# A selective-scan layer with a quantized feed-forward on one core: one order per chunk of a sequence, and bulk transfers issued behind the first chunk's C rows

## The chip, the cores and the metric

The kernel runs on 1 core of one Trainium2 chip. The metric is device time in microseconds (us), as the median of several executions. Four engines compute: TensorE (PE, with its weight loads shown apart as PEld), VectorE (DVE), ScalarE (ACT) and GpSimd (POOL). SyncE (SP) issues most of the DMAs. Each engine works through its own instruction list strictly in order; they meet only at semaphores.

## The reference, cut to what matters

The input x is 8 sequences of 2048 rows of 512 numbers.

```python
x = x + s6(layernorm(x))          # state space layer, 16 states per channel
#   xp = h @ x_proj_w.T           -> d_rank (64), B (16), C (16) for each row
#   delta = softplus(d_rank @ dt_proj_w.T + dt_proj_b)
#   for each state n:  s = exp(delta*A[n]) * s + delta*B[n]*h    (serial along the rows)
#   y = sum_n s_n * C[n]  + h * D
x = x + ffn(layernorm(x))         # int8 quantized matmul
#   x_scale = max|h| / 127 ; q = round(h / x_scale) ; out = (q @ weight_q.T) * x_scale * weight_scale + bias
```

## The kernel before

The 16384 rows are cut into 32 chunks of 512 rows, four to a sequence. A chunk's second step is 16 units, one for each state n; chunk p has units 16p to 16p+15. A unit goes through the engines like this:

- ACT (`decay`, L611) writes exp(delta*A[n]) into one of seven buffers A0 to A6, four pieces of 128x512. Unit s uses buffer A(s mod 7), which names the unit in the rows below.
- The term delta*B[n]*h is made with channels on partitions in one of three PSUM banks PB. For 10.5 of the 16 states ACT scales rows into DB (`act_b`, L632) and PE transposes them (`tb`, L777). For states 2, 5, 8, 11, 14 and half of 15, PE multiplies with a diagonal matrix DG (`tb`, L774), which is read back from a scratch tensor b_diag in device memory: SP writes B into its diagonals (`store_g`, L410) and loads them (`load_g`, L418). Off the diagonals b_diag is zero, written once at the start (L445).
- DVE (`scan`, L932) runs the recurrence over A in four pieces. In chunks 1 to 3 of a sequence it starts from CAR, the last column of the chunk before, which ACT copies (`carry`, L618); in chunk 0 it starts from zero, and after chunk 3 there is no copy.
- POOL (`times_c`, L546) multiplies the unit by C[n], broadcast to all partitions in CB. CB is loaded by SP for four states at once (`load_c`, L397) from c_rows, where `store_c` (L390) has put the chunk's C.
- PE (`th`, L799) transposes the unit back and adds it into Y.

Around these run the first layernorm and projections of the next chunk (`stats0`, `aggr0`, `log0`, `shift0`, `xn`, `x_t`, `xt_out`, `x_p`, `xp_out`, `b_c`, `bc_out`, `d_t`, `delta`, `dl_t`, `du`), and the second layernorm, quantization and matmul of the chunk before (`gather`, `square`, `var1`, `amax`, `root`, `inv`, `ascale`, `scales`, `step`, `centre`, `turn`, `qt_out`, `q_mm`, `scale_a`, `scale_p`, `add_c`). `add_b` and `add_c` are DMAs of POOL that add into the output.

The order on every engine is a table of numbers. `place` gives each task of chunk p the number 1000p plus its entry in PLACES; FIRST replaces the first entries for chunk 0, LAST those of chunk 31; `run` sorts. So all chunks but the first and last share one order, whatever their place in the sequence.

Before `run`, SP issues the loads of the first rows and weights, X1, two zero fills of b_diag (L445, 1.5 MB each), the quantized weights in two halves into C and DB2 (L449), ws, bias, its copy and X2. DVE's `weights` (L913) waits for all four of s_w2 and casts both halves.

Of the kernel before, what the change touches and what calls it, by code (L numbers as in the profile page):

```python
# [5 lines left out]
PERIOD = 1000  # L6
PLACES = {
        "act_b": (-188, -188, -123, -123, -121, -31, -25, -25, -10, 30, 38, 52, 143, 163, 166, 167, 167, 213,
        213, 235, 235, 235, 244, 244, 268, 308, 344, 344, 344, 441, 474, 531, 563, 588, 588, 595, 598, 625,
        626, 626, 714, 793),  # L10
        "add_b": (1370,),
        "add_c": (2141,),
        "aggr0": (-1339,),
        "amax": (1290,),
        "ascale": (1401,),
        "b_c": (-481,),
        "bc_out": (-526,),
        "bias_p": (20000, 20001, 20002, 20003),
        "carry": (60, 183, 215, 237, 251, 287, 314, 355, 468, 582, 651, 651, 693, 730, 916, 1005),
        "centre": (1446, 1465, 1481, 1481),  # L20
        "d_t": (-440, -423, -404, -391),
        "decay": (-248, -248, -229, -229, -45, 3, 10, 10, 92, 117, 136, 136, 136, 138, 151, 189, 192, 192,
        200, 200, 200, 200, 200, 200, 200, 200, 200, 241, 247, 247, 247, 265, 323, 323, 331, 331, 331, 331,
        369, 394, 439, 439, 439, 439, 549, 549, 549, 567, 641, 641, 654, 654, 658, 658, 658, 665, 665, 665,
        671, 671, 682, 684, 684, 727),
        "delta": (-428, -410, -395, -374),
        "dl_t": (-317, -149, -133, -122),
        "du": (-35, -33, -32, -30),
        "gather": (1172, 1172, 1173, 1173),
        "idle": (2244, 2663, 2696, 3192),  # L30
        "inv": (1291,),
        "last_p": (25000, 25001),
        "last_q": (885, 1247, 1323, 1493),
        "last_v": (30000, 30001),
        "load": (-2254,),
        "load_c": (91, 545, 545, 706),
        "load_g": (-320, -16, -2, 187, 679, 680),
        "log0": (-1232,),
        "put_last": (30000, 30001, 30002, 30003),
        "put_x": (1260,),  # L40
        "q_mm": (1883, 1894, 1928, 1946),
        "q_t": (201, 1218, 1342, 1469),
        "qt_out": (1825, 1825, 1937, 1937),
        "root": (1336,),
        "rstd0": (-1188,),
        "scale_a": (1948, 1973, 1982, 2042),
        "scale_out": (20000, 20001, 20002, 20003),
        "scale_p": (2083,),
        "scales": (1293,),
        "scan": (-9, -9, -9, 171, 171, 171, 171, 171, 171, 171, 171, 171, 172, 186, 212, 212, 212, 215, 215,  # L50
        215, 215, 215, 215, 215, 215, 215, 273, 281, 286, 289, 290, 292, 292, 292, 376, 376, 532, 532, 540,
        555, 592, 617, 617, 660, 660, 660, 661, 661, 668, 668, 866, 921, 921, 922, 922, 922, 962, 965, 967,
        969, 972, 972, 972, 984),
        "shift0": (-999,),
        "square": (1298, 1298, 1298, 1305),
        "stats0": (-2032, -2028, -2022, -1604),
        "step": (1442,),
        "store_c": (-276,),
        "store_g": (-322,),
# [8 lines left out]
        "times_c": (-187, 121, 353, 361, 361, 375, 404, 432, 442, 630, 763, 763, 763, 804, 808, 808),  # L68
        "turn": (1884,),
        "var1": (1317,),  # L70
        "weights": (-475,),
        "x_p": (-506, -503, -503, -487),
        "x_t": (-567, -557, -540, -531),
        "xn": (-783, -777, -767),
        "xn_p": (-641,),
        "xp_out": (-632,),
        "xt_d": (-1484, -1483),
        "xt_out": (-746, -725, -697, -692),
# [3 lines left out]
        "act_b": (-16343, -15473, -15469, -15107, -13275, -13273, -13174, -8291, -7133, -6341, -4257, -2015),  # L82
        "aggr0": (-3608,),
        "b_c": (-14522,),
        "bc_out": (-19425,),
        "carry": (-9543, -214),
        "d_t": (-14199, -14195, -13844, -13844),
        "decay": (-16453, -15024, -14020, -13332, -13332, -13332, -10585, -8244, -8243, -6057, -4718, -3029),
        "delta": (-19425, -18068, -18034, -18034),
        "dl_t": (-13844, -13844, -13844, -13844),  # L90
        "du": (-987, -941, -941, -665),
        "load": (16363,),
        "load_c": (-13005, -6878, -2125, -1821),
# [65 lines left out]
def build(nc, cs, dg, b4, x, a_log, d_skip, wxp, wdt, dt_b, wq, ws, bias, out):  # L159
# [36 lines left out]
    with ctx:  # L196
# [844 lines left out]
```

## Time and profile before

| | us |
|---|---|
| median of 3 runs (2790.3 to 2793.21) | 2790.7 |
| the profiled execution | 2791.34 |
| its span, first to last instruction | 2789.6 |
| busy in the span: PE / DVE / ACT / POOL | 2746.0 / 2711.7 / 2694.8 / 2689.7 |
| PE weight loads busy | 2516.2 |
| instructions PE / DVE / ACT / POOL | 22516 / 2801 / 4927 / 980 |
| mean granted TensorE clock | 0.996 of full speed |
| moved by DMA | 344.33 MB, mean 123 GB/s |

In the 40 slices of the span all four engines stand at nine tenths or more from the second slice to the last but one. A row of waits names the engine that waited and its line, then what released it, with the total, the count and the longest. In a timeline row the bracket is the idle time ahead of the group and its releaser. PE's busy time has modelled ends, so a PE that is always busy need not be at its full pace.

### The profile page before, as it was taken

To read this page: it belongs to the slowest core of one execution; us is meant where nothing else is said; L and a number is where in the kernel's file an instruction comes from. 1 tells how busy PE (TensorE), PEld (TensorE's weight loads), DVE (VectorE), ACT (ScalarE), POOL (GpSimd) and SP (SyncE) were. 2 spreads that over 40 slices of the span, in tenths; PEclk is the share of its full clock that TensorE was granted. 3 is DMA by queue.
4 is the path that set the end of the run, shared out by engine and by line. 5 is a ranking of instruction groups with operands and counts; after the bars stand their busy time and mean duration, and the time that the engine had idled before them with its cause. 6 is when DMAs were issued, how large, how long until landed. Compare 5 with 4: busy or idle time off the path is not lost.

```text
span 2789.6 us, 59136 instructions
## 1 busy us (share of the span) xinstructions
PE 2746.0 (98%) x22516; PEld 2516.2 (90%) x22516; DVE 2711.7 (97%) x2801; ACT 2694.8 (97%) x4927; POOL 2689.7 (96%) x980
## 2 busy tenths in 40 slices
PE   7999999999999999999999999999999999999998
PEld 6899999899998999998999989999989999999987
DVE  6999999999999999999999999999999999999987
ACT  7999999999999999999999999999999999999994
POOL 4899999999999999999999999999999999999998
PEclk9999999999999999999999999999999999999999
DMA  5245454465454554444654545545446544464442
GB/s 199 78 125 130 124 127 117 112 149 124 109 139 105 138 130 123 128 121 109 153 122 107 139 104 139 130 126 125 121 109 149 123 109 137 104 140 115 122 122 54
DMA packets 271653, 344.33 MB, mean 123 GB/s; under 512 B 174917, under 2 KB 174917, under 8 KB 251018
## 3 DMA queue, kind: packets, MB, share of 16 engines
q1 hardware_dynamic: 250538, 275.54, 34.8%
q0 software_dynamic: 20832, 65.02, 13.1%
q8 instruction: 178, 2.92, 0.4%
q14 instruction: 105, 0.86, 0.1%
HBM read 253.60 MB, written 103.16 MB: 128 GB/s over the span
## 4 chain that ended last, share of the span: by engine, by line
PE 36%; POOL 21%; ACT 15%; DMA 12%; issue 12%; DVE 4%; SPq 1%; POOLq 0%; ACTq 0%; DVEq 0%
POOL A L546 18%; PE Y L799 11%; PE PB L774 8%; DMA out<-C 8%; PE PB L777 8%; ACT A L611 7%; ACT DB L632 3%; DVE A L932 3%; DMA CB<-c_rows 2%; ACT C L661 2%; PE PM L858 2%; POOL C L563 2%; PE PM L839 2%; PE PM L899 1%; PE Y L795 1%
## 5 line engine op out<-in xcount | busy, mean ns | idle before, releaser
L546 POOL TENSOR_TENSOR A<-A,CB 128x2048 f32<-128x2048 f32 x511 | 2336.3, 4602 | 58.9 <-ACT CAR L618 29.0
L932 DVE TENSOR_TENSOR_SCAN A<-A,CAR,PB 128x512 f32<-128x512 f32 x1536 | 1832.7, 1259 | 13.2 <-PE PB L777 8.3
L611 ACT ACTIVATE A<-DEL,an 128x512 f32<-128x512 f32 x2048 | 1311.7, 712 | 5.5 <-PE Y L799 5.1
L799 PE MATMUL Y<-idf,A 128*128 128x128 f32 x8192 | 1091.5, 273 | 0.0
L799 PEld LDWEIGHTS Y<-idf,A 128*128 128x128 f32 x8192 | 938.4, 141 | 34.2 <-issue 16.4
L632 ACT ACTIVATE DB<-XN,BC 128x512 f32<-128x512 f32 x1344 | 897.4, 712 | 7.8 <-DVE XN L962 5.2
L777 PE MATMUL PB<-idf,DB 128*128 128x128 f32 x5376 | 763.6, 274 | 19.2 <-DVE A L932 12.0
L774 PEld LDWEIGHTS PB<-DG,XN 128*128 128x128 f32 x5632 | 687.0, 192 | 87.0 <-issue 79.1
L774 PE MATMUL PB<-DG,XN 128*128 128x128 f32 x5632 | 729.6, 277 | 1.2 <-DVE A L932 0.6
L777 PEld LDWEIGHTS PB<-idf,DB 128*128 128x128 f32 x5376 | 619.5, 142 | 37.3 <-DVE A L932 12.4
L932 DVE TENSOR_TENSOR_SCAN A<-A,PB 128x512 f32<-128x512 f32 x512 | 584.3, 1200 | 23.6 <-PE PB L774 13.3
L563 POOL TENSOR_TENSOR C<-C,wsb 128x2048 f32<-128x2048 f32 x31 | 142.1, 4583 | 0.0
L795 PE MATMUL Y<-dd,XT 128*128 128x128 f32 x1024 | 137.2, 278 | 3.1 <-POOL A L546 3.1
L858 PE MATMUL PM<-XP,wds 97*128 97x512 f32 x248 | 131.9, 613 | 1.0 <-ACT DEL L722 1.0
L795 PEld LDWEIGHTS Y<-dd,XT 128*128 128x128 f32 x1024 | 126.1, 194 | 3.8 <-POOL A L546 3.8
L899 PE MATMUL PM<-wqb,QT 128*128 128x512 bf16 x496 | 127.7, 380 | 0.8 <-ACT C L731 0.7
L839 PE MATMUL PM<-XT,wxs 128*96 128x512 f32 x256 | 120.1, 592 | 0.0
L661 ACT ACTIVATE C<-X,SX 128x512 f32<-128x512 f32 x124 | 88.2, 713 | 14.2 <-DMA out<-C 13.9
L555 POOL TENSOR_SCALAR C<-X,SX,AM 128x512 int16<-128x512 f32 x124 | 93.2, 761 | 0.1
L731 ACT ACTIVATE C<-PM,AM 128x512 f32<-128x512 f32 x124 | 84.5, 681 | 5.4 <-PE PM L899 4.9
L950 DVE BATCH_NORM_STATS2 ST<-X 128x6 f32<-128x512 f32 x128 | 83.7, 675 | 4.8 <-DMA X<-in_x 4.8
L940 DVE SCALAR_TENSOR_TENSOR X<-Y,X 128x512 f32<-128x512 f32 x128 | 82.5, 678 | 3.8 <-PE Y L799 3.8
(92 smaller groups left out, 1371.1 us busy)
## 6 DMA issues: line engine op xcount, KB each, us to landing
CB<-c_rows SPq DMA_DIRECT2D x128, 1024.0 KB, 6.1
DG<-b_diag SPq DMA_DIRECT2D x192, 256.0 KB, 3.0
X<-in_x SPq DMA_DIRECT2D x31, 1024.0 KB, 7.8
out<-X SPq DMA_DIRECT2D x31, 1024.0 KB, 5.1
out<-bias_rows POOLq DMA_DIRECT2D x31, 1024.0 KB, 8.1
out<-C POOLq DMA_DIRECT2D x31, 1024.0 KB, 12.1
b_diag<-DG SPq DMA_DIRECT2D x2, 1536.0 KB, 11.7
b_diag<-BC SPq DMA_DIRECT2D x192, 2.0 KB, 2.5
```

The source lines that it names most:

```text
L546: gp.tensor_tensor(A[s % NA][:, :, :], A[s % NA][:, :, :], CB[:, s % (4 * NG), :].unsqueeze(1).broadcast_to([128, KB, L]), ALU.mult).then_ ...
L563: gp.tensor_tensor(C[:, :, :], C[:, :, :], wsb[:, :].unsqueeze(1).broadcast_to([128, T, D]), ALU.mult)\
L611: act.activation(A[s % NA][:, g, :], DEL[k % 2][:, g, :], ACT.Exp, scale=an[:, g, n:n + 1])\
L632: i = act.activation(DB[m % ND][:, j, :], XN[k % 2][:, j, :], ACT.Copy, scale=BC[k % 2][:, j, n:n + 1])
L774: i = pe.matmul(PB[u % NPB][:, j * 128:(j + 1) * 128], XN[k % 2][:, j, g * 128:(g + 1) * 128], DG[:, (NDG * k + DIAG.index(n)) % NR, j, :] ...
L777: i = pe.transpose(PB[u % NPB][:, j * 128:(j + 1) * 128], DB[(scaled(s) - 1) % ND][:, j, g * 128:(g + 1) * 128], idf[:, :])
L795: i = pe.matmul(Y[j][:, g * 128:(g + 1) * 128], XT[:, g, j * 128:(j + 1) * 128], dd[:, g, :], start=(g == 0), stop=False, skip_group_check ...
L799: i = pe.matmul(Y[j][:, g * 128:(g + 1) * 128], A[s % NA][:, g, j * 128:(j + 1) * 128], idf[:, :], is_transpose=True, start=False, stop=(n ...
L839: i = pe.matmul(PM[0:96, :], wxs[:, g, :], XT[:, g, :], start=(g == 0), stop=(g == KB - 1))
L858: pe.matmul(bank(p, g)[:, :], wds[:, g * 128:(g + 1) * 128], XP[:, :], start=True, stop=True)\
L899: i = pe.matmul(bank_q(p, j)[:, :], QT[:, j, g, :], wqb[:, g, :], start=(g == 0), stop=(g == KB - 1))
L932: dve.tensor_tensor_scan(A[s % NA][:, g, :], A[s % NA][:, g, :], PB[(4 * s + g) % NPB][:, :], init, ALU.mult, ALU.add).then_inc(s_scan, 1)
```

## The change

1. PLACES holds four orders instead of one, one for each chunk of a sequence: `place` adds the entry of chunk p mod 4 to the start of the sequence. FIRST now places nearly every task of chunk 0, and LAST has new numbers.
2. SP's start is cut. Of the bulk only X1 and the first zero fill stay ahead of chunk 0's work. A new task `late` issues the rest from inside the order: first half of the quantized weights, second zero fill, second half, and then ws, bias and its copy. X2 becomes a placed load.
3. Both halves of the quantized weights go through C, one after the other; DB2 is not used. `weights` is two tasks on DVE, each waiting for its own half, and the wait of ACT's `act_b` for it is gone. The second half's load waits for the first cast.
4. The second zero fill reads a second cleared buffer of DG (one more memset on POOL), so the load that reuses that buffer waits for the fill. The two fills have a semaphore each.
5. ws and bias have a semaphore of their own, s_w3, waited for by `scale_p` and `bias_p`.

```diff
-            return PERIOD * p + PLACES[name][i]
+            return PERIOD * CPB * (p // CPB) + PLACES[name][p % CPB * count(name) + i]
...
-        "inv": (1291,),
+        "inv": (1184, 2337, 3169, 4124),
-        "ascale": (1401,),
+        "ascale": (1314, 2298, 3257, 4345),
...
-                if p == 0:
-                    sp.wait_ge(s_zd, 32)
+                if p <= 1:
+                    sp.wait_ge(s_zd[p], 16)
...
             load(1)
-            sp.wait_ge(s_zero, 1)
-            for i in range(2):
-                sp.dma_start(dg[i, ...], DG[:, 0, ...]).then_inc(s_zd, 16)
-            for h, stage in enumerate((C, DB[2])):
-                sp.dma_start(stage..., wq[256 * h:256 * h + 256, :]...).then_inc(s_w2, 16)
-            sp.dma_start(wsb[:, :], ws.partition_broadcast(128)).then_inc(s_w2, 16)
-            sp.dma_start(bib[:, :], bias.partition_broadcast(128)).then_inc(s_w2, 16)
-            sp.dma_start(b4[:, :], bias.partition_broadcast(4)).then_inc(s_b4, 16)
-            load(2)
+            sp.wait_ge(s_zero, 2)
+            blank(0, 0)
+
+            def late(p, i):
+                if p:
+                    return
+                if i == 1:
+                    blank(1, NR - 1)
+                elif i < 3:
+                    h = i // 2
+                    if h:
+                        sp.wait_ge(s_wb, 1)
+                    sp.dma_start(C..., wq[256 * h:256 * h + 256, :]...).then_inc(s_w2, 16)
+                else:
+                    sp.dma_start(wsb[:, :], ws.partition_broadcast(128)).then_inc(s_w3, 16)
+                    sp.dma_start(bib[:, :], bias.partition_broadcast(128)).then_inc(s_w3, 16)
+                    sp.dma_start(b4[:, :], bias.partition_broadcast(4)).then_inc(s_b4, 16)
...
-                dve.wait_ge(s_w2, 64)
-                for h, stage in enumerate((C, DB[2])):
+                dve.wait_ge(s_w2, 16 * (h + 1))
```

**The start on SP.** Its list in the kernel before, from X1 to the first load of DG (the zero fill is b_diag<-DG, `store_c` c_rows<-XP, `store_g` b_diag<-BC0):

```order
L378 DMA X1<-in_x 128x4x512
L445 DMA b_diag<-DG 768x1x512 x2
L449 DMA C<-in_wq 128x2x512
L449 DMA DB2<-in_wq 128x2x512
L451 DMA wsb<-in_ws 128x512
L452 DMA bib<-in_bias 128x512
L453 DMA bias_rows<-in_bias 4x512
L378 DMA X2<-in_x 128x4x512
L390 DMA c_rows<-XP 16x512
L397 DMA CB<-c_rows 128x2048
L410 DMA b_diag<-BC0 128x4x1 x6
L418 DMA DG<-b_diag 128x512
```

The same stretch of the changed kernel, up to ws:

```order
L491 DMA X1<-in_x 128x4x512
L551 DMA b_diag<-DG 768x1x512
L503 DMA c_rows<-XP 16x512
L523 DMA b_diag<-BC0 128x4x1 x6
L510 DMA CB<-c_rows 128x2048
L533 DMA DG<-b_diag 128x512 x3
L575 DMA C<-in_wq 128x2x512
L551 DMA b_diag<-DG 768x1x512
L510 DMA CB<-c_rows 128x2048 x2
L533 DMA DG<-b_diag 128x512 x3
L575 DMA C<-in_wq 128x2x512
L578 DMA wsb<-in_ws 128x512
```

The stores of C and B, the first load of C and three loads of DG now stand ahead of the quantized weights and the second fill; the stores of B come ahead of the load of C.

**The start on PE.** After the transposes of states 0 and 1, before (PB0 to PB2 are the scan's banks, L774 the products with DG for state 2, L795 and L799 the sums of unit 0 into Y, which need POOL's first product):

```order
L777 MATMUL PB1<-idf,DB1 128x128 x4
L795 MATMUL Y0<-dd,XT 128x128 x4
L799 MATMUL Y0<-idf,A0 128x128 x4
L795 MATMUL Y1<-dd,XT 128x128 x4
L799 MATMUL Y1<-idf,A0 128x128 x4
L795 MATMUL Y2<-dd,XT 128x128 x4
L799 MATMUL Y2<-idf,A0 128x128 x4
L774 MATMUL PB2<-DG,XN0 128x128 x4
L774 MATMUL PB0<-DG,XN0 128x128 x4
L774 MATMUL PB1<-DG,XN0 128x128 x4
L795 MATMUL Y3<-dd,XT 128x128 x4
```

The same place of the changed kernel:

```order
L902 MATMUL PB1<-idf,DB1 128x128 x4
L899 MATMUL PB2<-DG,XN0 128x128 x4
L899 MATMUL PB0<-DG,XN0 128x128 x4
L899 MATMUL PB1<-DG,XN0 128x128 x4
L899 MATMUL PB2<-DG,XN0 128x128 x4
L902 MATMUL PB0<-idf,DB2 128x128 x4
L920 MATMUL Y0<-dd,XT 128x128 x4
L924 MATMUL Y0<-idf,A0 128x128 x4
L902 MATMUL PB1<-idf,DB2 128x128 x4
L902 MATMUL PB2<-idf,DB2 128x128 x4
L920 MATMUL Y1<-dd,XT 128x128 x4
```

The four products of state 2 stood behind three quarters of unit 0's sums and one stood behind all four; now all four stand ahead of the first.

**The quantization of a chunk, DVE and POOL.** DVE in chunk 9 of the kernel before, where the maximum (TENSOR_REDUCE) and the two reciprocals of chunk 8 stand. The scans are printed as SCALAR_TENSOR_TENSOR; A4 is unit 151, A5 unit 152:

```order
L932 SCALAR_TENSOR_TENSOR A4<-A4,CAR,PB1 128x512
L932 SCALAR_TENSOR_TENSOR A4<-A4,CAR,PB2 128x512
L973 TENSOR_REDUCE PW<-C 128x4
L932 SCALAR_TENSOR_TENSOR A4<-A4,CAR,PB0 128x512
L979 RECIPROCAL RO<-RO 128x4
L932 SCALAR_TENSOR_TENSOR A4<-A4,CAR,PB1 128x512
L932 SCALAR_TENSOR_TENSOR A5<-A5,CAR,PB2 128x512
L932 SCALAR_TENSOR_TENSOR A5<-A5,CAR,PB0 128x512
L985 RECIPROCAL AM<-AM 128x4
L932 SCALAR_TENSOR_TENSOR A5<-A5,CAR,PB1 128x512
```

The same in the changed kernel:

```order
L1056 SCALAR_TENSOR_TENSOR A5<-A5,CAR,PB2 128x512
L1056 SCALAR_TENSOR_TENSOR A5<-A5,CAR,PB0 128x512
L1056 SCALAR_TENSOR_TENSOR A5<-A5,CAR,PB1 128x512
L1097 TENSOR_REDUCE PW<-C 128x4
L1056 SCALAR_TENSOR_TENSOR A5<-A5,CAR,PB2 128x512
L1103 RECIPROCAL RO<-RO 128x4
L1056 SCALAR_TENSOR_TENSOR A6<-A6,CAR,PB0 128x512
L1056 SCALAR_TENSOR_TENSOR A6<-A6,CAR,PB1 128x512
L1056 SCALAR_TENSOR_TENSOR A6<-A6,CAR,PB2 128x512
L1056 SCALAR_TENSOR_TENSOR A6<-A6,CAR,PB0 128x512
```

The first reciprocal stands one unit and a quarter later. Of the other three chunks of a sequence, the two next ones have three scans between the maximum and the reciprocal, and the last has none. POOL at the same chunk before, where PW<-PW,RO is the first instruction of `ascale` and waits for the reciprocal (A2 is unit 149, A3 unit 150):

```order
L546 TENSOR_TENSOR A1<-A1,CB 128x2048
L572 DMA out_0<-bias_rows 128x2048
L546 TENSOR_TENSOR A2<-A2,CB 128x2048
L515 TENSOR_TENSOR PW<-PW,RO 128x4
L517 TENSOR_TENSOR RO<-PW,RO 128x4
L520 TENSOR_TENSOR AM<-RO 128x4
L524 TENSOR_SCALAR AM<-AM 128x4
L546 TENSOR_TENSOR A3<-A3,CB 128x2048
```

And in the changed kernel (A4 is unit 151):

```order
L673 TENSOR_TENSOR A2<-A2,CB 128x2048
L673 TENSOR_TENSOR A3<-A3,CB 128x2048
L673 TENSOR_TENSOR A4<-A4,CB 128x2048
L642 TENSOR_TENSOR PW<-PW,RO 128x4
L644 TENSOR_TENSOR RO<-PW,RO 128x4
L647 TENSOR_TENSOR AM<-RO 128x4
L651 TENSOR_SCALAR AM<-AM 128x4
L673 TENSOR_TENSOR A5<-A5,CB 128x2048
```

`ascale` moved from behind unit 149 to behind unit 151.

**Counts of the order that the prediction uses** (steady chunks, in units ahead of or behind the first unit of the chunk concerned). ACT writes the last two normalized pieces (`xn`) of the first chunk of a sequence 7.5 units of decays ahead of that chunk's first decay, where it was 9.2; PE's first transpose of them (`x_t`) stands 8.8 units of PB products ahead of the chunk's first, where it was 10.0. `add_c` stands behind unit 17 on POOL for three chunks of four, where it was behind unit 18. The first `square` stands on ACT behind 25.0, 23.8, 24.5 and 24.0 units for the four chunks, where it was 24.0. In chunk 0 of the program, the copy of CAR for unit 0 stands behind 18 activations of `decay` and `act_b` on ACT, where it was 14. In the last chunk three scans and more now stand between the maximum and the second reciprocal of the chunk before, where there was none.

## Rows read from the trace of the kernel before

**Rows 1.** The engines by stage: us, busy (instructions), clock, DMA share, GB/s.

```profile
0.00:174.00 174.00, 155.72 (x1177) 138.96 (x1178) 145.37 (x158) 151.82 (x279) 122.15 (x55) 0.96 0.43 133
174.00:2615.00 2441.00, 2429.75 (x20065) 2233.83 (x20064) 2416.28 (x2494) 2411.30 (x4409) 2404.53 (x858) 1.00 0.49 125
2615.00:2790.00 175.00, 160.50 (x1279) 143.39 (x1276) 150.07 (x151) 131.63 (x242) 163.06 (x69) 0.98 0.40 97
```

**Rows 2.** The one ACT copy QT of each chunk 0 to 30: first and last start.

```profile
L744 ACT ACTIVATE QT<-C x31: 1892/1894/1912, 195.2 to 2736.6; 128x2048 bf16<-128x2048 int16 x31
```

**Rows 3.** Timeline at 1000 us, PE groups: start, length, line, count.

```profile
1005.47 0.60 PE L777 MATMUL PB<-idf,DB 128*128 128x128 f32 x4
1000.71 1.04 PE L777 MATMUL PB<-idf,DB 128*128 128x128 f32 x8
```

**Rows 4.** Waits in 174 to 2615 us, DVE: total, times, longest.

```profile
DVE A L932 <- PE PB L777: 8.6, 27, 1.0
DVE RO L979 <- ACT RO L680: 7.7, 18, 0.7
DVE A L932 <- PE PB L774: 4.2, 13, 0.4
```

**Rows 5.** Waits in 174 to 2615 us, POOL and ACT.

```profile
POOL PW L515 <- DVE RO L979: 16.5, 23, 1.9
...
ACT C L661 <- DMA out<-C: 13.9, 18, 1.7
```

**Rows 6.** Timeline of the start, SP: issue, time spent issuing.

```profile
17.34 1.74 SPq L390 DMA_DIRECT2D c_rows<-XP  x1
29.45 0.33 SPq L397 DMA_DIRECT2D CB<-c_rows  x1
29.91 4.83 SPq L410 DMA_DIRECT2D b_diag<-BC  x6
37.82 0.33 SPq L418 DMA_DIRECT2D DG<-b_diag  x1
```

**Rows 7.** Timeline of the start, DVE, with the idle time ahead.

```profile
26.05 0.70 DVE L913 CAST wqb<-C 128x1024 bf16<-128x1024 int32 x1 [0.21 <-DMA bib<-in_bias]
27.56 4.52 DVE L932 TENSOR_TENSOR_SCAN A<-A,PB 128x512 f32<-128x512 f32 x4
33.75 4.55 DVE L932 TENSOR_TENSOR_SCAN A<-A,PB 128x512 f32<-128x512 f32 x4 [1.67 <-PE PB L777]
38.22 1.85 DVE L950 BATCH_NORM_STATS2 ST<-X 128x6 f32<-128x512 f32 x3
46.62 3.44 DVE L932 TENSOR_TENSOR_SCAN A<-A,PB 128x512 f32<-128x512 f32 x3 [6.55 <-PE PB L774]
```

**Rows 8.** Timeline of the start, POOL.

```profile
34.42 9.02 POOL L546 TENSOR_TENSOR A<-A,CB 128x2048 f32<-128x2048 f32 x2 [21.33 <-DMA CB<-c_rows]
52.61 4.54 POOL L546 TENSOR_TENSOR A<-A,CB 128x2048 f32<-128x2048 f32 x1 [9.02 <-ACT CAR L618]
```

**Rows 9.** Timeline of the start, ACT: twelve decays in a row.

```profile
43.77 7.44 ACT L611 ACTIVATE A<-DEL,an 128x512 f32<-128x512 f32 x12
```

**Rows 10.** Timeline near the end, DVE.

```profile
2698.34 2.29 DVE L973 TENSOR_REDUCE PW<-C 128x4 f32<-128x2048 f32 x1 [1.20 <-ACT C L661]
2701.71 0.18 DVE L979 RECIPROCAL RO<-RO 128x4 f32<-128x4 f32 x1 [1.09 <-ACT RO L680]
2703.16 0.18 DVE L985 RECIPROCAL AM<-AM 128x4 f32<-128x4 f32 x1 [1.27 <-POOL AM L524]
```

**Rows 11.** DVE alone, up to its first scan: us, busy (instructions), clock, DMA.

```profile
0.00:27.56 27.56, 10.92 (x25) 0.99 0.95 333
```

**Rows 12.** 0 to 1085 us of one line each: ACT L611, PE L777, PE L774.

```profile
0.00:1085.00 1085.00, 512.15 (x800) 0.99 0.49 127
0.00:1085.00 1085.00, 297.87 (x2084) 240.93 (x2084) 0.99 0.49 127
0.00:1085.00 1085.00, 281.23 (x2176) 264.69 (x2176) 0.99 0.49 127
```

More of the change, by code:

```diff
@@ L69 @@
[L69 to L78, printed above, removed]
+        "act_b": (-185, -157, -116, -116, -116, -100, -100, -100, -22, -21, 37, 41, 41, 117, 170, 170, 170,
[9 rows of a table added]
+        "add_b": (1179, 2335, 3286, 4433),
+        "add_c": (2211, 2980, 3953, 4858),
@@ new lines @@
+        "scale_a": (1874, 1892, 1968, 2011, 2834, 2846, 2876, 2900, 3910, 3972, 3998, 4098, 4842, 4868, 4893,
+        4972),
+        "scale_out": (20000, 20001, 20002, 20003, 21000, 21001, 21002, 21003, 22000, 22001, 22002, 22003,
+        23000, 23001, 23002, 23003),
+        "scale_p": (2040, 2824, 3901, 4646),
+        "scales": (1462, 2461, 3455, 4129),
+        "scan": (67, 70, 70, 70, 70, 70, 70, 70, 74, 74, 82, 82, 108, 108, 108, 108, 108, 108, 108, 121, 121,
[15 rows of a table added]
+        "square": (1338, 1350, 1358, 1413, 2270, 2270, 2270, 2404, 3281, 3288, 3302, 3314, 4271, 4290, 4295,
@@ new lines @@
+        "add_b": (1318,),
+        "add_c": (2152,),
+        "aggr0": (-3991,),
+        "amax": (1162,),
+        "ascale": (1353,),
+        "b_c": (-29593,),
+        "bc_out": (-37985,),
+        "carry": (-17572, -11784, -8330, -7126, -2374, -1596, -971, 250, 257, 411, 579, 581, 657, 723, 853,
+        983),
+        "centre": (1515, 1537, 1553, 1553),
+        "d_t": (-29593, -29239, -23167, -19278),
+        "decay": (-29823, -25234, -25234, -24834, -21839, -19600, -19222, -17824, -16853, -16413, -16118,
[4 rows of a table added]
@@ new lines @@
+        "delta": (-36568, -36568, -35326, -31640),
+        "dl_t": (-18780, -18099, -18099, -16168),
+        "du": (-1402, -1306, -1306, -1306),
+        "gather": (1117, 1117, 1125, 1126),
+        "inv": (1207,),
+        "late": (-12995, -12985, 100, 200),
+        "load": (16363,),
+        "load_c": (-34082, -7485, -6765, 435),
+        "load_g": (-30274, -17300, -16756, -4842, -4602, -852),
+        "log0": (-83651,),
+        "put_x": (1716,),
+        "q_mm": (1845, 1857, 1876, 1884),
@@ new lines @@
+        1002, 1005, 1012, 1013, 1013, 1013),
+        "shift0": (-88312,),
+        "square": (1117, 1184, 1319, 1329),
+        "stats0": (-56459, -46320, -38392, -34964),
+        "step": (1379,),
+        "store_c": (-44487,),
+        "store_g": (-39959,),
[9 rows of a table added]
+        "times_c": (-11758, -8632, -4412, -3209, -1284, -523, -412, 53, 86, 199, 227, 227, 227, 227, 294, 515),
+        "turn": (2007,),
+        "var1": (1363,),
+        "weights": (-100, 300),
+        "x_p": (-30660, -29608, -29608, -29603),
@@ L255, in build @@
         s_zero = sem("s_zero")
-        s_zd = sem("s_zd")
+        s_zd = [sem(f"s_zd{i}") for i in range(2)]
         s_ae = sem("s_ae")
@@ L332, in bank_q, with count @@
             return PM if p < END else Y[j]
+        def count(name):
+            return len(PLACES[name]) // CPB
         def place(name, i, p):
@@ L480, in _ @@
             gp.memset(DG[:, 0, :, :], 0.0).then_inc(s_zero, 1)
+            gp.memset(DG[:, NR - 1, :, :], 0.0).then_inc(s_zero, 1)
             gp.memset(one[:, :], 1.0).then_inc(s_big, 1)
@@ L1010, in _ @@
                 scale_out=scale_out, inv=lambda p, i: inv(p), scales=lambda p, i: scales(p),
-                weights=lambda p, i: weights(p), last_q=last_q, scan=scan)
+                weights=weights, last_q=last_q, scan=scan)
 _INS = ["x", "a_log", "d_skip", "wxp", "wdt", "dt_b", "wq", "ws", "bias"]
```

230 lines of the change are left out of this document (114 added, 116 removed), and 114 rows, old and new, of tables (FIRST, LAST, PLACES).

## The prediction

> **What bounds the kernel now.** I read the page's busy shares first, then the engines by stage. The reader is to see that no engine stands out. From 174 to 2615 us [rows 1] DVE is idle for 2441.00 - 2416.28 = 24.7 us, ACT for 29.7, POOL for 36.5, and PE, whose ends are modelled, for 11.3. The chunks pass at (2736.6 - 195.2)/30 = 84.7 us each [rows 2], of which 83.8 are DVE's work (98.99%). So a new order, which takes away no work, can give the middle at most DVE's 24.7 us. The other idle time is at the two ends: DVE 28.6 us before 174 us and 24.9 us after 2615 us [rows 1].
>
> For PE the busy time is not its pace: four transposes take 0.60 us and eight take 1.04 [rows 3], so one more costs 0.11 us. The 20065 instructions of the middle at that pace are 2207 us, a lower bound, since some have four times the columns. PE's slack in the middle is between 11.3 and 234 us. I take DVE as the tightest.
>
> Had PE's 11.3 us been the limit, the middle could give no more than that. The Trainium skill (Perfetto Trace Analysis, Identifying the Most-Contended Engine) says that matmul occupancy is no good measure and that weight-load occupancy is to be used. Here that is 2233.83/2441 = 91.5% against 99.5% for matmuls; by it PE has room, and the limit stays DVE's 24.7 us.
>
> Then the waits of the middle. DVE waits for the first reciprocal's input 7.7 us in 18 places, and for PE's banks 8.6 + 4.2 us [rows 4]. POOL waits for that same reciprocal 16.5 us; ACT waits 13.9 us for the accumulating store of the chunk before [rows 5]. In the start I read SP, DVE and POOL side by side: C is stored at 17.34 but can be loaded only at 29.45, and B's diagonals at 37.82 [rows 6]; POOL starts at 34.42, and DVE stands for 1.67 and 6.55 us [rows 7, 8].
>
> **The start.** SP first. The store of C is issued at 17.34 and takes 1.74, to 19.1. The six stores of B now follow at once, 4.83 us, to 23.9; the first load of C is issued there, if the store has landed. Before, 12.1 us passed from store to load, with two fills and four bulk loads queued ahead. The load took 34.42 - 29.45 = 5.0 us to POOL's start [rows 6, 8], so C is there at about 29. The loads of DG could start 37.82 - (29.91 + 4.83) = 3.1 us after the last store of B [rows 6]; that is now 27.0 instead of 37.8.
>
> POOL: its first product was held by C until 34.42. Now it is held by the copy of CAR. Unit 0's scans end at 27.56 + 4.52 = 32.1 [rows 7], but on ACT the copy stands behind four more activations at 7.44/12 = 0.62 us [rows 9]: 32.1 + 2.5 = 34.6. So the earlier C wins nothing on POOL's first unit; it is cover for what follows.
>
> DVE: its stall of 6.55 us was PE, which had state 2's products behind three sums of unit 0, and these behind POOL's first product. In the new order the products stand first and need only DG, issued at 27.0. That stall goes, and the 1.67 us too, since ACT's last piece for unit 1 no longer stands behind the copy of CAR. Of DVE's 28.6 us of idle before 174 us [rows 1], 27.56 - 10.92 = 16.6 lie ahead of the first scan [rows 11]; less the two stalls, 3.8 us are left in small waits, and they may go too. With 0.3 us for the cast and aggregation that stood ahead of the first scan this is 12.3 us at most. Against it stands DVE work that was free inside idle time and now lies between scans: four statistics of X1 and three of X2 at 1.85/3 = 0.62 us, two casts at 0.65, an aggregation at 0.3 [rows 7]; together 5.9 us. Net 6.4 at best. What is late next is the first cast: it follows eight scans and four statistics, at about 39 us, and needs half the weights, whose load is issued after the three of DG, about 28 us. If it takes 14 us, DVE stands 3 us. I take 4.0 gained; bounds: 6.4 gained, 3 lost. The added memset (0.5 us) runs on an idle POOL, nothing; uncovered it would cost 0.5. Moving ws, bias and X2 back costs nothing: their readers come some tens of us later. The new waits of the second half (on the first cast) and of DG's fourth buffer (on the second fill) have some 20 us of cover; behind them on SP stand the loads of ws, bias and X2, which are not near.
>
> **The middle.** DVE's 7.7 us come from one scan between maximum and reciprocal (0.43 us each). In the new order two chunks of four have three scans there, so nothing is left; one has one scan as before; one has none, which costs some 1.1 us by the place near the end where none stands between either [rows 10]. That last one lies in a sequence's first chunk, whose scans without CAR are shorter, and where DVE waits for PE anyway. So I count 7.7 less a quarter, 5.8 us gained; if the scan-less one counts in full, 7 x 1.1 = 7.7 us eat it up.
>
> POOL: before, `ascale` behind unit 149 needed DVE through three quarters of unit 151, 1.75 units ahead; now behind 151 it needs unit 152, 1.0 ahead. Three quarters of a unit are 4 us, against waits of at most 1.9 [rows 5]: the 16.5 us go. ACT: `add_c` starts one unit, 5.3 us, earlier in three chunks of four, and `square` hardly moves; waits of at most 1.7 us [rows 5] go. These 30 us are not on DVE, but they are what makes PE's banks late for it now and then: of DVE's 12.8 us for banks I count a fifth, 2.7. Together 8.5 us; bounds: 0 and 20.
>
> **The end.** DVE stood with nothing between: 1.20, 1.09 and 1.27 us [rows 10]. Now scans stand there. Of 3.6 us I count 1.5, since the last chunk has other waits behind; bounds 0 and 3.6.
>
> **Sum.** 4.0 + 8.5 + 1.5 = 14.0 us. The profiled execution took 2791.34 (span 2789.6 and 1.7 around it), so 2777.3; the median is 0.6 us below it: 2776.7, say 2777.
>
> **Rivals.**
> - Full engines (the middle gives nothing): with four engines at 98.5% and more, a wait taken away on one turns up on another. For it: idle is only 1%, and spread over many waits under 1 us. Against: the two largest, POOL's and ACT's, have a plain cause in the order. Then 4.0 + 1.5 gained: 2785.2.
> - Nearly all goes: 6.4 + 20 + 3.6: 2760.7. For it: four orders can follow the lighter scans and the missing copies of CAR. Against: 0.15 us of idle a chunk is little for lists in fixed order.
> - Slower: PE stands for the normalized rows of a sequence's first chunk. Up to 1085 us ACT has done 800/4 = 200 units of decays and PE (2084 + 2176/2)/16 = 198.25 units of products (those with DG are two instructions each) [rows 12], so ACT leads by 1.75 units. The new order needs 8.8 - 7.5 = 1.3 units there, where it needed 0.8, plus the two pieces, about 0.3: 1.6. The margin is 0.15 unit, 0.8 us. If the new order makes the lead 1.25, PE stops 0.35 unit, 1.8 us, at seven places, and everything behind it in its list with it: the banks for DVE first. That costs 12.9 us and the 8.5 are not won: 2790.7 + 12.9 - 5.5 = 2798. It decides from a stop of about 0.8 us each. Against it: the lead can be as much as the ring of seven buffers allows.
> - That the change doesn't do what it says I exclude: the order shows every move.
>
> **How the numbers follow.** Forecast 0.50, full engines 0.28, nearly all 0.12, slower 0.10. A measurement of this kernel tells 0.2% (5.6 us) from no change, so faster is below 2785.1 and slower above 2796.3; only the stopped PE lies beyond that. Of full engines half falls on each side of 2785.1: faster 0.50 + 0.12 + 0.14 = 0.76, same 0.14, slower 0.10. The forecast's own bounds are 2770 to 2784. The range runs from the near half of "nearly all", 2763, to just above the time of before, 2791, where the start loses its 3 us and the middle wins little; it leaves out about 0.06 below and 0.10 above.
>
> **What would show it.** In the profile after: DVE's first scan at 27 to 28 us, no stall above 3 us behind unit 1, the load of C near 24 us and that of DG near 27; POOL's wait for the reciprocal under 5 us in the middle, ACT's for the store under 3; DVE idle of 14 to 18 us in the same 2441 us and chunks at 84.4 us. Wrong would be: a wait of PE's x_t for ACT's XN of a us or more, once in a sequence; DVE idle unchanged with the named waits gone (full engines); or a cast that waits for its weights.

## The result and the profile after

The changed kernel takes 2779.22 us (median of 5 runs, 2777.97 to 2779.38) against 2790.7 (5 runs, 2787.25 to 2793.21): a ratio of 0.9958, 95% interval 0.9944 to 0.9973. It is 11.5 us faster. The profiled execution took 2779.38 us, its span is 2777.6. The forecast of 2777 was 2 us off.

The engines by stage, after, in the columns of [rows 1]. The last row ends where the span ends; the same row of before is set beside it from the span's end there.

```profile
0.00:174.00 174.00, 157.34 (x1199) 140.46 (x1200) 149.79 (x160) 154.79 (x284) 126.34 (x59) 0.96 0.44 137
174.00:2615.00 2441.00, 2433.24 (x20141) 2241.91 (x20140) 2423.53 (x2502) 2419.07 (x4426) 2413.39 (x859) 1.00 0.49 125
2615.00:2777.65 162.65, 149.21 (x1182) 131.55 (x1179) 138.39 (x141) 121.66 (x219) 151.87 (x65) 0.98 0.41 101
```

```profile
2615.00:2789.61 174.61, 160.50 (x1279) 143.39 (x1276) 150.07 (x151) 131.63 (x242) 163.06 (x69) 0.98 0.40 98
```

DVE's idle time, by stage: 28.6 us became 24.2 at the start (4.4 won), 24.7 became 17.5 in the middle (7.2), 24.5 became 24.3 at the end (0.3). Together that is the whole difference between the two profiled executions, 11.96 us. It has to be: DVE's busy time in the whole span is 2711.7 in both, so what its idle time lost the span lost. This says where the time went and not which engine set it. At 83.8 us of DVE work a chunk now passes in 83.8 x 2441.00 / 2423.53 = 84.4 us.

Waits in 174 to 2615 us, after, DVE, POOL and ACT in turn, to be read beside [rows 4, 5]:

```profile
DVE RO L1103 <- ACT RO L805: 6.0, 7, 0.9
DVE A L1056 <- PE PB L899: 4.5, 14, 0.5
DVE A L1056 <- PE PB L902: 2.1, 10, 0.6
...
POOL AM L657 <- DVE AM L1109: 7.2, 7, 1.4
...
ACT C L856 <- PE PM L1024: 6.1, 9, 0.8
```

POOL's 16.5 us for the reciprocal and ACT's 13.9 us for the accumulating store are gone. DVE's wait for the reciprocal's input, 7.7 us in 18 places, is 6.0 in 7: once in a sequence, where no scan stands between maximum and reciprocal. DVE's waits for PE's banks fell from 12.8 to 6.6 us. In their place POOL waits for the second reciprocal, 7.2 us in 7 places, and ACT for PE.

The start, after. SP, then DVE, then POOL, to be read beside [rows 6 to 8]:

```profile
18.19 3.12 SPq L523 DMA_DIRECT2D b_diag<-BC  x6
21.36 0.50 SPq L510 DMA_DIRECT2D CB<-c_rows  x1
25.27 1.28 SPq L533 DMA_DIRECT2D DG<-b_diag  x3
26.60 0.48 SPq L575 DMA_DIRECT2D C<-in_wq  x1
```

```profile
27.31 4.55 DVE L1056 TENSOR_TENSOR_SCAN A<-A,PB 128x512 f32<-128x512 f32 x4 [2.08 <-PE PB L902]
32.66 2.33 DVE L1056 TENSOR_TENSOR_SCAN A<-A,PB 128x512 f32<-128x512 f32 x2 [0.80 <-ACT A L738]
...
39.51 0.67 DVE L1037 CAST wqb<-C 128x1024 bf16<-128x1024 int32 x1
40.09 3.55 DVE L1056 TENSOR_TENSOR_SCAN A<-A,PB 128x512 f32<-128x512 f32 x3
44.13 2.33 DVE L1056 TENSOR_TENSOR_SCAN A<-A,PB 128x512 f32<-128x512 f32 x2 [0.49 <-PE PB L899]
...
78.57 2.58 DVE L1037 CAST wqb<-C 128x1024 bf16<-128x1024 int32 x1
```

```profile
34.63 4.54 POOL L673 TENSOR_TENSOR A<-A,CB 128x2048 f32<-128x2048 f32 x1 [21.54 <-ACT CAR L745]
43.91 4.58 POOL L673 TENSOR_TENSOR A<-A,CB 128x2048 f32<-128x2048 f32 x1 [4.74 <-ACT CAR L745]
```

No stall above 1 us is left on DVE between 33 and 98 us, where 6.55 us stood. POOL starts as late as before and is now released by the copy of CAR. The first cast waits for nothing; the second takes 2.58 us where it took 0.69.

PE's clock has a part in this stretch. In the kernel before it was granted half of full speed, the lower of its two levels (1.2 of 2.4 GHz), from 39.00 to 44.00 us, in the columns of [rows 1]:

```profile
39.00:44.00 5.00, 5.00 (x23) 5.00 (x24) 1.07 (x2) 5.00 (x9) 4.60 (x2) 0.50 0.99 377
```

PE had stood 2.86 us for POOL's first product just ahead of it, with the clock at the lower level already, and had no gap in these 5 us, after which the clock was full. The 36 matmuls of three quarters of unit 0's sums took 6.46 us there, 39.00 to 45.46; at 0.11 us each [rows 3] they would take 4.0. So some 2.5 us of DVE's 6.55 were the clock (an estimate from these numbers). The changed kernel has the lower level as well, from 38.53 to 44.02, where 24 products with DG take 5.49 us:

```profile
38.53 5.49 PE L899 MATMUL PB<-DG,XN 128*128 128x128 f32 x24 [2.26 <-DVE A L1056]
```

They are ahead of DVE's scans, and DVE waits only 0.49 us for them.

### The profile page after: what moved, and what is told of

Read it like the earlier page. It is cut to its first block, busy times and chain, and to the rows that moved or that the text cites. A ratio compares the mean times of both kernels' runs of the same rounds, so it can differ in the third digit from the quotient of the medians.

```text
span 2777.6 us, 59139 instructions
## 1 busy us (share of the span) xinstructions
PE 2739.8 (99%) x22516; PEld 2513.9 (91%) x22516; DVE 2711.7 (98%) x2801; ACT 2695.5 (97%) x4927; POOL 2691.6 (97%) x981
## 4 chain that ended last, share of the span: by engine, by line
PE 87%; ACT 5%; DVE 4%; issue 2%; POOL 1%; DMA 1%; SPq 1%; DVEq 0%; POOLq 0%; ACTq 0%
PE Y L924 28%; PE PB L899 21%; PE PB L902 19%; PE Y L920 4%; PE PM L1024 4%; PE PM L983 4%; PE PM L964 3%; DVE A L1056 3%; ACT A L738 3%; PE PM L992 2%; PE PM L954 2%; ACT DB L757 1%; POOL A L673 1%; DVE XN L1086 0%; DMA b_diag<-BC 0%
## 5 line engine op out<-in xcount | busy, mean ns | idle before, releaser
L738 ACT ACTIVATE A<-DEL,an 128x512 f32<-128x512 f32 x2048 | 1330.1, 712 | 6.7 <-PE Y L924 6.1
L924 PE MATMUL Y<-idf,A 128*128 128x128 f32 x8192 | 1071.2, 273 | 1.3 <-POOL A L673 1.2
```

What stands on the lines that cost most here:

```text
L738: act.activation(A[s % NA][:, g, :], DEL[k % 2][:, g, :], ACT.Exp, scale=an[:, g, n:n + 1])\
L924: i = pe.matmul(Y[j][:, g * 128:(g + 1) * 128], A[s % NA][:, g, j * 128:(j + 1) * 128], idf[:, :], is_transpose=True, start=False, stop=(n ...
```

## The experiments

In the expectations "after" is the changed kernel. The kernel before was timed anew with each group, on the same chip as the group, so the ratios are what compares.

**The transfers, the tables, the bulk, the quantization.** Four kernels; the kernel before took 2789.98 us beside them. The first has the new start on SP with the numbers of before:

```diff
 # on the changed kernel
+PLACES.update(<the numbers of the kernel before, for each of the four chunks>)
+FIRST, LAST: the numbers of the kernel before, with
+    'late': (-2600, -2590, 100, 200), 'weights': (-100, 300)
+    load(2) placed at -2585
```

> The changed program (bulk behind chunk 0's rows of C, weights in halves through C) with the tables of the kernel before; only the late transfers are placed anew. Theory (the transfers alone are worth little, since in the old order PE has state 2's products behind POOL's first product): POOL's first product starts at 32 to 33 us instead of 34.42, DVE's stall of 6.55 us shrinks to about 4, the cast and statistics now lie between scans, the middle is as before: 2788 to 2791 us. Rival (the early C and DG are what won the time): 2779 to 2783 us, the stall gone.

Measured: 2802.22 us, ratio 1.0045 (1.0032 to 1.0057), 12 us slower than before. DVE stood 10.12 us before the second cast, whose weights were issued only at 83.31. That is mostly the place where I put it, not the change; the last group repeats this run without it.

The second has the start and FIRST of before, and the new PLACES and LAST:

```diff
 # on the kernel before
-            return PERIOD * p + PLACES[name][i]
+            return PERIOD * CPB * (p // CPB) + PLACES[name][p % CPB * count(name) + i]
+PLACES, LAST: the numbers of the changed kernel
```

> The program before with its own start (bulk first, its own FIRST table) and the four orders and LAST of the changed kernel. Theory (about 7 us in the middle and under 1 at the end come from the orders by themselves): 2781 to 2785 us, DVE idle 17 to 18 us in 174 to 2615 us, the stall of 6.55 us at the start unchanged. Rival (the middle gains only because the start comes out in better step): 2788 to 2791 us.

Measured: 2782.2 us, ratio 0.997 (0.9959 to 0.9982). DVE is busy for 2423.36 of the middle's 2441 us, as in the changed kernel (2423.53). The orders by themselves are worth about 8 us.

The third is the changed kernel with the bulk back at the head of SP's list (only the second half of the weights stays late, behind the first cast):

```diff
             blank(0, 0)
+            blank(1, NR - 1)
+            sp.dma_start(C..., wq[0:256, :]...).then_inc(s_w2, 16)
+            sp.dma_start(wsb[:, :], ws.partition_broadcast(128)).then_inc(s_w3, 16)
+            ...
+            load(2)
```

> The changed kernel with the second fill, the first half of the quantized weights, ws, bias and X2 issued at the head again; the tables unchanged. Theory (the new order of chunk 0 needs DG early): C is loaded near 27 us, DG lands after 33, DVE stands some 5 to 7 us more behind unit 1: 2783 to 2787 us. Rival (the order of chunk 0 alone made the gain of the start): 2779 to 2780 us.

Measured: 2779.6 us, ratio 0.9958 (0.9945 to 0.9972), the same as the changed kernel. Its SP at the start, its DVE behind unit 1, and its PE at the first products of state 2:

```profile
18.82 9.96 SPq L523 DMA_DIRECT2D b_diag<-BC  x6
28.97 0.36 SPq L510 DMA_DIRECT2D CB<-c_rows  x1
32.01 1.28 SPq L533 DMA_DIRECT2D DG<-b_diag  x3
```

```profile
39.93 0.70 DVE L1044 CAST wqb<-C 128x1024 bf16<-128x1024 int32 x1
40.54 8.98 DVE L1063 TENSOR_TENSOR_SCAN A<-A,PB 128x512 f32<-128x512 f32 x8
49.80 6.78 DVE L1063 TENSOR_TENSOR_SCAN A<-A,PB 128x512 f32<-128x512 f32 x6 [0.27 <-PE PB L909]
```

```profile
36.57 1.13 PE L906 MATMUL PB<-DG,XN 128*128 128x128 f32 x8 [1.03 <-DMA DG<-b_diag]
```

C is loaded 7.6 us later and DG 6.7 us later than in the changed kernel, and the time is the same. POOL starts at 35.53, held by C, 0.9 us later than there; PE stands 1.03 us for DG, to 36.57, and its products are still ahead of DVE's scan of unit 2 at 40.54. So holding back the bulk, which half of the change is about, wins nothing here.

One thing this run does not undo: the stores of B still stand ahead of the load of C. DG is issued at 32.01, where the kernel before issued it at 37.82. No run has the new order on PE with DG as late as that. From issue to product it took 36.57 - 32.01 = 4.6 us; from 37.82 that gives 42.4, and with 1.1 us for a quarter's eight matmuls DVE would stand some 3 us at unit 2 (an estimate).

The fourth takes the kernel before and moves the quantization's steps by hand, with one order for all chunks:

```diff
+MOVED = {'amax': 1293, 'inv': 1500, 'scales': 1536, 'ascale': 1433, 'step': 1443, 'root': 1438}
+            if p < END - 1 and name in MOVED:
+                return PERIOD * p + MOVED[name]
```

> The kernel before with one part of the new order: for chunks 0 to 29 ascale on POOL behind unit 151 instead of 149 (in the numbers of chunk 8), the first reciprocal on DVE behind 152 with two scans after the maximum, root, scales and step moved with them. Theory (these waits were paid in time): DVE's wait for RO goes from 7.7 to under 2 us in the middle, POOL's from 16.5 to under 6: 2783 to 2788 us. Rival (full engines: a wait taken away turns up elsewhere): the waits go, DVE idle stays at 24 to 25 us, 2790 to 2792 us.

Measured: 2871.47 us, ratio 1.029, 80 us slower. Two rows of its waits in the middle:

```profile
ACT PW L683 <- DVE PW L978: 69.1, 27, 2.6
...
DVE A L937 <- PE PB L779: 47.8, 97, 2.2
```

DVE's wait for the reciprocal went, as meant, and ACT, whose `root` now came up before DVE had the maximum, stood up to 2.6 us in each of 27 places; the decays behind it, CAR and PE's banks came late in turn. A wait of 7.7 us was traded for 65 us more on DVE.

**PE's order, two more moves, and more work for PE.** The kernel before took 2791.11 us beside these. First, the changed kernel with state 2's four products put back behind the sums of unit 0, on PE alone:

```diff
+FIRST["tb"][8:12] = (-6200, -6200, -6200, -5660)   # and the next ones not before -5655
```

> The changed kernel with one thing of chunk 0 undone: on PE state 2's products stand again behind the sums of unit 0 (three behind three of them, one behind all four), as in the kernel before. Theory (the start's gain is this order on PE, since with the bulk sent first it was as large): PE waits for POOL's first product, DVE stands 5 to 8 us behind unit 1, and of that 4 to 6 us reach the end: 2783 to 2786 us. Rival (the new order on ACT and DVE made it): 2779 to 2781 us.

Measured: 2785.88 us, ratio 0.998 (0.9971 to 0.9989): 0.0022 of 2790, 6 us, is lost again. PE, then DVE:

```profile
39.61 2.08 PE L923 MATMUL Y<-dd,XT 128*128 128x128 f32 x8 [4.10 <-POOL A L676]
...
46.16 2.84 PE L902 MATMUL PB<-DG,XN 128*128 128x128 f32 x24
```

```profile
47.32 3.44 DVE L1059 TENSOR_TENSOR_SCAN A<-A,PB 128x512 f32<-128x512 f32 x3 [6.75 <-ACT A L741]
```

The stall is back at 6.75 us, though C and DG come as early as in the changed kernel. (The bracket names ACT; PE's products for that scan start only at 46.16.) So PE's order is needed for the gain of the start, and with it the bulk can stay at the head. How early DG has to be is open, as said above.

Two moves on top of the fourth kernel: `root` at 1440, and then `add_c` at 2090 as well.

> As e4_quant_moved (the quantization's scalar chain of the kernel before moved later, as the new orders have it), but with ACT's root six activations later too, so that it stands behind the maximum. In e4 ACT stood 69 us for the maximum in 27 places and the time rose by 81 us. Theory (waits on a nearly full engine are paid): ACT's wait for the maximum under 2 us in all, DVE's for RO none, POOL's 4 to 5 us instead of 16.5: 2784 to 2788 us. Rival (full engines): waits gone, 2790 to 2792 us.

Measured: 2848.15 us, ratio 1.0204 (1.019 to 1.0218). ACT's wait went from 69.1 to 2.2 us and 23 us came back; 57 stayed. DVE waits 29.7 us for PE's banks and 24.4 for decays. Neither theory of mine had this.

> e4b_quant_root_late plus add_c one unit earlier on POOL, so that the accumulating store starts 5 us sooner. Theory: ACT's 13.9 us of waiting for it fall under 3, and one to three us more are won than in e4b: 2782 to 2786 us. Rival (ACT is not what bounds): same time as e4b within 1 us.

Measured: 2838.85 us, ratio 1.0173 (1.0159 to 1.0187). Storing a unit earlier is worth 9.3 us on top, and ACT's wait for the store is gone; on the packed order of before both moves together still lose. What part of the middle's gain each single wait brought was not to be had this way.

Last in this group, more work for PE. In the changed kernel three quarters of state 15 in place of a half go through the diagonal matrix: each chunk has four 128x128 matmuls more on PE and one activation less on ACT.

```diff
-    ROWS = {2: 4, 5: 4, 8: 4, 11: 4, 14: 4, 15: 2}
+    ROWS = {2: 4, 5: 4, 8: 4, 11: 4, 14: 4, 15: 3}
```

> The changed kernel with three instead of two row blocks of state 15 made by PE's products with DG (two instructions each) instead of ACT's scaling and one transpose: per chunk PE has 4 instructions of 0.11 us more (14 us in all), ACT one activation of 0.61 us less (20 us in all). If PE's pace bounds: 2789 to 2794 us. If ACT bounds: 2765 to 2776. If neither (DVE, or the order of all): 2777 to 2783.

Measured: 2796.61 us, ratio 1.0016 (1.0001 to 1.0031), against 0.9958 for the changed kernel: 0.0058 of 2790, 16 us more. The middle, in the columns of [rows 1], and three of its waits:

```profile
174.00:2615.00 2441.00, 2428.07 (x20088) 2236.40 (x20087) 2411.13 (x2485) 2386.73 (x4361) 2393.72 (x855) 1.00 0.49 124
```

```profile
ACT C L861 <- PE PM L1029: 33.0, 44, 1.3
...
POOL A L678 <- DMA CB<-c_rows: 16.2, 7, 4.0
...
DVE A L1061 <- PE PB L907: 11.8, 37, 1.5
```

ACT has less to do and DVE the same, and both wait more for PE than in the changed kernel. The size fits too: 32 x 4 x 0.11 = 14 us is PE's added work at the pace of [rows 3]. But it is not PE alone. POOL now stands 16.2 us for the load of C's rows, where it stood 2.1, and between the two profiled executions PE's busy time in the whole span grew by 12.0 us (2739.8 to 2751.7) and its idle time by 6.3. All other tasks kept their places, as in the runs that moved single steps. So the run shows that this order has no room for 14 us more on PE, and not that PE's pace sets the time.

**The transfers alone, PE relieved, two touches.** The kernel before took 2792.3 us beside these. The first run again without its misplaced cast:

```diff
 # on the first kernel of the experiments
-    load(2) placed at -2585
+    load(2) placed at -2602
-    'weights': (-100, 300)
+    'weights': (-100, 1000)
```

> The changed kernel's SP start (bulk behind chunk 0's rows of C, C and B stored first), with the tables of the kernel before; X2 is loaded ahead of the quantized weights and the second cast of them stands after unit 1's period, so that neither makes DVE stand among its first scans. My prediction said that DVE's 6.55 us stall behind unit 1 would go because DG is issued earlier. If that is what the start's gain comes from: 2782 to 2786 us, with the DVE stall behind unit 1 under 2 us. If it comes from PE's order (state 2's products ahead of unit 0's sums), the transfers alone are worth at most 2 us: 2788 to 2792, with DVE still standing 5 us or more behind unit 1.

Measured: 2793.66 us, ratio 1.0006 (0.9997 to 1.0015), no change. DVE and POOL at the start:

```profile
33.80 4.55 DVE L1065 TENSOR_TENSOR_SCAN A<-A,PB 128x512 f32<-128x512 f32 x4 [1.68 <-PE PB L911]
40.61 3.46 DVE L1046 CAST wqb<-C 128x1024 bf16<-128x1024 int32 x1 [2.25 <-DMA C<-in_wq]
...
45.78 21.20 DVE L1065 TENSOR_TENSOR_SCAN A<-A,PB 128x512 f32<-128x512 f32 x19
```

```profile
32.45 4.54 POOL L682 TENSOR_TENSOR A<-A,CB 128x2048 f32<-128x2048 f32 x1 [19.52 <-ACT CAR L754]
38.96 4.56 POOL L682 TENSOR_TENSOR A<-A,CB 128x2048 f32<-128x2048 f32 x1 [1.96 <-ACT CAR L754]
```

I expected DVE to stand 5 us behind unit 1, and it doesn't. From the end of unit 1's scans to the next scan it is 7.4 us (38.35 to 45.78) and was 8.3 (38.30 to 46.62), and a wait for the weights, a slow cast and the statistics fill it. The next scans start 0.8 us earlier; the second cast takes 2.79 us, 2.1 more than before, and so costs more than that. State 2's products on PE, before and here:

```profile
45.46 2.84 PE L774 MATMUL PB<-DG,XN 128*128 128x128 f32 x24
```

```profile
42.94 2.84 PE L908 MATMUL PB<-DG,XN 128*128 128x128 f32 x24
```

They start 2.5 us earlier, since POOL's first product starts 2.0 us earlier. So in the old order the earlier transfers do shorten PE's delay; what they cost on DVE takes the gain back.

Then the counterpart of the run with more rows through the diagonal: `15: 1` in place of `15: 2`.

> The changed kernel with three quarters instead of a half of state 15 multiplied as rows by ACT: in each chunk one activation more on ACT (0.61 us) and four 128x128 matmuls fewer on PE. Three quarters the other way round cost 17.4 us, 0.54 us a chunk. If PE's pace alone sets the chunk and ACT's 17.5 us of middle idle are room: 32 x 0.5 = 16 us less, 2763 to 2770. If ACT bounds as soon as PE is relieved: its 32 x 0.61 = 19.5 us more work against about 22 us of idle in the middle is just about all the room there is, and its waits for PE's banks and delta stay, so 2783 to 2796. If DVE bounds (my prediction): no change but for what ACT makes late, 2778 to 2784, with DVE's idle in the middle as after, 17.5 us.

Measured: 2787.08 us, ratio 0.9983 (0.9974 to 0.9992): 0.0025 of 2790, 7 us more than the changed kernel.

```profile
174.00:2615.00 2441.00, 2421.43 (x19891) 2219.12 (x19948) 2416.92 (x2495) 2428.41 (x4437) 2406.66 (x857) 1.00 0.49 124
```

ACT's idle time in the middle is down to 12.6 us from 21.9, every other engine's is up. So less work on PE wins nothing while ACT gets 20 us more. Of the three splits of state 15 half is the best, in an order that was made for half.

> The changed kernel with four numbers of PLACES altered: the first reciprocal of the chunk without a scan between maximum and reciprocal stands later, and the chain of POOL and the scales behind it are moved to fit. It is aimed at DVE's 6.0 us of wait for RO and POOL's 7.2 us of wait for the scales. If waits on DVE and POOL are paid in time: 2773 to 2777. If PE's pace sets the chunk, both waits go and nothing is won: 2778.5 to 2781.

```diff
+PLACES.update({'inv': (1184, 2337, 3169, 4125), 'scales': (1293, 2461, 3455, 4340), 'ascale': (1314, 2298, 3257, 4355)})
```

Measured: 2787.78 us, ratio 0.9986 (0.9977 to 0.9995), 8 us slower than the changed kernel. In its middle:

```profile
DVE AM L1112 <- POOL AM L654: 9.4, 7, 1.8
POOL AM L660 <- DVE AM L1112: 9.1, 14, 1.3
```

The 6.0 us for RO went, and the next link of the same chain took 9.4 us: the second reciprocal, now a scan's length from the first, comes before POOL's four small steps are done. Neither theory allowed for that, so it doesn't tell them apart. It also sizes what four altered numbers can do to such an order: 8 us, as much as less work on PE cost and half of what more work cost.

> The changed kernel with one number of FIRST altered: ACT's copy of unit 1's last column stands earlier in chunk 0, so that POOL's second product does not wait 4.74 us for it at 43.9 us. If POOL's start is on the path: 2776 to 2777.5. If PE's order sets the start (as the run with PE's products put back says), POOL's wait shrinks by 2 us or more and the time stays: 2778 to 2780.

```diff
-FIRST["carry"] = (-17572, -11784, ...)
+FIRST["carry"] = (-17572, -14270, ...)
```

Measured: 2778.82 us, ratio 0.9952 (0.994 to 0.9965), within the changed kernel's interval.

```profile
41.87 4.57 POOL L676 TENSOR_TENSOR A<-A,CB 128x2048 f32<-128x2048 f32 x1 [2.31 <-ACT CAR L748]
49.34 9.08 POOL L676 TENSOR_TENSOR A<-A,CB 128x2048 f32<-128x2048 f32 x2 [2.90 <-ACT CAR L748]
```

POOL's second product starts 2.0 us earlier and its third waits the longer; POOL is not on the path there. No version that was run beats the changed kernel by more than the measurement can tell.

## Why the prediction was right, and where it was not

**The sum.** 14.0 us forecast, 11.5 measured: 4.0 against 4.4 at the start, 8.5 against 7.2 in the middle, 1.5 against 0.3 at the end. The cause named, the order of the lists, was right; that the sum came so near is in part luck, as the shares below show. (A fifth of 12.8 us is also 2.6, and not 2.7.)

**The start: PE's order was right, the late bulk was not needed.** C was loaded at 21.4 and DG at 25.3, near the 24 and 27 forecast; POOL began at 34.63, forecast 34.6, released by CAR as said; the first cast stood at 39.51, forecast 39, but did not wait. The step "in the new order the products stand first and need only DG, issued at 27.0" held in its first half: with PE's order put back the stall is back at 6.75 us, though DG is early. Its second half asked for more than was needed: with DG issued at 32.0 the time is the same (third run). Whether 37.82, as before, would do is not shown, and my estimate says no. Holding back the bulk is worth nothing, and the transfers alone nothing either. What I left out is the clock: 2.5 us of the stall, by the estimate above, came from PE's sums at half speed. And two errors cancelled. I counted up to 3 us of waiting for the first cast's weights, which did not come. I priced both casts at 0.65 us each from a place where POOL stood idle, and the second took 2.58.

**The middle: the total near by luck, the shares not.** I counted 5.8 us for the reciprocal's input and 2.7 for PE's banks. Measured: 1.7 and 6.2. The step "That last one lies in a sequence's first chunk ... so I count 7.7 less a quarter" failed: a chunk without a scan between costs its full wait, 0.86 us in each of 7 places, cheap scans or not. My bound for it (7 x 1.1) was the value to take. The long waits of POOL and ACT went as forecast (16.5 and 13.9 us to none), and the banks came in time more often than I allowed. Whether the one caused the other was only argued: the runs that moved the steps one by one disturbed the order too much to show it.

**"I take DVE as the tightest": not borne out, and not refuted.** Four short matmuls a chunk more cost 16 us, while by my bounds PE had up to 234 us of room in the middle. That bound was loose, and the trace of before could have told me. There six fp32 matmuls of 128x512 take 2.74 us and two take 1.02, so one more costs 0.43, and in four bf16 ones of that width, 1.03 us with 0.38 for one alone, one more costs 0.22. The middle has 452 and 464 of these. Counted so, PE's 20065 instructions are 2207 + 452 x 0.32 + 464 x 0.11 = 2403 us, an estimate, and its room is 38 us, beside 24.7 on DVE, 29.7 on ACT and 36.5 on POOL. All four engines are within 1.6% of the middle.

The profile's chain that ended last, by engine, of before and of after:

```profile
PE 36%; POOL 21%; ACT 15%; DMA 12%; issue 12%; DVE 4%; SPq 1%; POOLq 0%; ACTq 0%; DVEq 0%
```

```profile
PE 87%; ACT 5%; DVE 4%; issue 2%; POOL 1%; DMA 1%; SPq 1%; DVEq 0%; POOLq 0%; ACTq 0%
```

It looks like a proof that PE took over, and isn't one. The run with both moves, 48 us slower than the kernel before and with DVE idle for 67 us of the middle, has PE at 84%, and the run with the bulk first, as fast as the changed kernel, has 75%. The Trainium skill (Perfetto Trace Analysis, Identifying the Most-Contended Engine) has TensorE's headroom judged by MFU and the busy share of weight loads. That share, 91.5%, leaves 207 us in the middle; the count of instructions at their pace leaves 38. ACT is as near: 20 us more work for it cost 7 us even with PE relieved. Which engine is the tightest stays open: more work on PE, more on ACT and four altered numbers all lost time, and in none of these runs was the order made anew. The "full engines" rival was right about how near the limit is, but it did not cap the gain.

**The end.** The waits of 1.20, 1.09 and 1.27 us around the maximum of the last chunk but one went, and DVE stands for ACT elsewhere, here 20 us ahead of that maximum:

```profile
2666.39 1.28 DVE L1056 TENSOR_TENSOR_SCAN A<-A,CAR,PB 128x512 f32<-128x512 f32 x1 [1.88 <-ACT A L738]
2668.89 10.65 DVE L1056 TENSOR_TENSOR_SCAN A<-A,CAR,PB 128x512 f32<-128x512 f32 x9 [1.21 <-ACT A L738]
```

**The rivals.** PE did not stand for XN of a sequence's first chunk: the waits of the middle hold no such row for PE's x_t (L954). Nearly all of the idle time did not go: 17.5 us of 24.7 are left. Full engines is out by the 7.2 us of the middle, and by the run with the orders alone.

## What to carry to other kernels

Before a stall is put down to a late transfer, move the transfer alone and the order alone: here the stall came back with the instruction order of the engine in between, and holding back the bulk won nothing. Then look at what the run with the other order still has of the transfers: here DG was still earlier than before. In these lists, packed to 99%, steps of the quantization moved by themselves pushed the wait to the next link of their chain, for 0.3 to 3% more time; the orders that won were tables for all tasks. Giving one engine a little more work in such a list tests the list as much as the engine. And where the work of an engine is the same in two runs, its idle time accounts for the difference and does not explain it.

## What the runs showed of the hardware

In these traces a cast on DVE that meets a product on POOL ends about 0.55 us behind that product, as if it had waited for it, and the profile counts all of it as DVE's busy time. The bf16 cast of 128x1024 took 0.67 to 0.70 us where POOL was idle, and in the changed kernel 2.58 us at 78.57. POOL there:

```profile
76.04 14.02 POOL L673 TENSOR_TENSOR A<-A,CB 128x2048 f32<-128x2048 f32 x3 [2.25 <-ACT CAR L745]
```

The first product, of 4.56 us, ends at 80.60, and the cast at 81.15, 0.55 later. With the bulk first:

```profile
75.84 13.99 POOL L680 TENSOR_TENSOR A<-A,CB 128x2048 f32<-128x2048 f32 x3 [2.24 <-ACT CAR L752]
...
78.05 2.89 DVE L1044 CAST wqb<-C 128x1024 bf16<-128x1024 int32 x1
```

Here the product, of 4.55 us, ends at 80.39 and the cast at 80.94, 0.55 later. With the transfers alone the product at 38.96, of 4.56 us, ends at 43.52 and the cast of 3.46 us at 44.07, 0.55 later. In turn POOL's three products take 14.02 and 13.99 us with a cast among them, and 13.62 without. The Trainium skill (SBUF — State Buffer, Who interferes with whom) says that a DVE cast in its two-port mode and a GpSimd instruction share a port pair that one of them holds for its whole instruction. The ends in these traces agree; in which mode the cast ran they do not show.

The issue of B's six small stores took 3.12 us behind one fill (changed kernel), 4.84 with the load of C just ahead of them (transfers alone), and 9.96 with two fills, half of the weights, ws, the biases and X2 ahead (bulk first).
